# A gated recurrent layer on one core: TensorE's step loop made one loop of 128 rounds, VectorE's loop turned, weights loaded by row quarters, the opening reordered

## The reference

```
vz, vr, vh = cond @ C_z + b_z, cond @ C_r + b_r, cond @ C + b
xz, xr, xh = x @ W_z, x @ W_r, x @ W          # for every step t
h = 0
for t in range(512):
    z = sigmoid(xz[t] + h @ U_z + vz)
    r = sigmoid(xr[t] + h @ U_r + vr)
    c = tanh(xh[t] + (r * h) @ U + vh)
    h = (1 - z) * h + z * c
    out[t] = x[t] + h
```

## Time and profile before

| | |
|---|---|
| median of 3 runs | 2264.65 us (2261.95 to 2265.0) |
| the profiled execution | 2264.97 us |
| its span | 2263.1 us |
| PE busy | 2185.4 us (97%), 107502 products |
| PEld busy | 1797.5 us (79%) |
| DVE, ACT, POOL busy | 1754.5, 1326.6, 687.8 us |

### The profile page before, as it was taken

The page is one execution under the profiler, slowest core; times in us unless marked ns, Lnnn a source line. Parts: engine busy times, 40 slices in busy tenths (PEclk is TensorE's granted clock), DMA queues, the critical chain, the costliest instruction groups (busy, mean ns, idle before and its releaser), DMA issues.

```text
span 2263.1 us, 238050 instructions
## 1 busy us (share of the span) xinstructions
PE 2185.4 (97%) x107502; PEld 1797.5 (79%) x107502; DVE 1754.5 (78%) x8226; ACT 1326.6 (59%) x4623; POOL 687.8 (30%) x1546
## 2 busy tenths in 40 slices
PE   2899999999999999999999999999999999999996
PEld 1788878888888887888888888788878888888875
DVE  5687878778778777777777777777777877877874
ACT  3566556566566665666656666556656656656652
POOL 0233333333333333333333333333333333333331
PEclk9999999999999999999999999999999999999998
DMA  9110110110110110111101101101101101101101
GB/s 196 34 38 19 38 38 19 38 37 19 38 33 23 38 35 22 38 29 28 38 24 33 38 24 32 38 19 37 38 19 38 38 19 38 38 20 38 28 11 22
DMA packets 145390, 78.48 MB, mean 35 GB/s; under 512 B 9024, under 2 KB 140608, under 8 KB 145216
## 3 DMA queue, kind: packets, MB, share of 16 engines
q1 hardware_dynamic: 145216, 76.84, 14.1%
HBM read 43.25 MB, written 33.55 MB: 34 GB/s over the span
## 4 chain that ended last, share of the span: by engine, by line
PE 95%; issue 2%; SPq 1%; DMA 1%; DVE 0%; ACT 0%; DVEq 0%; POOLq 0%; POOL 0%
PE p_bank L269 44%; PE c_bank L259 20%; PE banks L297 16%; PE banks L306 15%; SPq L152 1%; DMA x_nat<-in_x_dram 1%; SPq L147 0%; SPq L163 0%; PE p_bank L278 0%; DVE taken L631 0%; DVE state L635 0%; DVE h_t L639 0%; ACT gate_c L430 0%; SPq L155 0%; DVE h_lo L597 0%
## 5 line engine op out<-in xcount | busy, mean ns | idle before, releaser
L269 PE MATMUL p_bank<-w_hi,x_t 128*32 128x384 f16 x16384 | 1183.1, 327 | 2.4 <-issue 1.6
L269 PE MATMUL p_bank<-w_lo,x_t 128*32 128x384 f16 x8192 | 701.7, 327 | 2.2 <-issue 2.2
L269 PEld LDWEIGHTS p_bank<-w_hi,x_t 128*32 128x32 f16 x16384 | 462.3, 97 | 155.2 <-issue 1.5
L259 PEld LDWEIGHTS c_bank<-u,reset_t 128*32 128x32 f32 x32704 | 488.4, 110 | 98.6 <-DVE reset_t L611 71.7
L259 PE MATMUL c_bank<-u,reset_t 128*32 128x64 f32 x32704 | 551.0, 219 | 8.4 <-issue 8.1
L230 POOL TENSOR_TENSOR result<-x_nat,state 128x128 f32<-128x128 f32 x512 | 233.9, 457 | 1010.0 <-DVE h_lo L597 1008.4
L423 ACT ACTIVATE gate_r<-banks,gates_down 128x64 f32<-128x64 f32 x1024 | 265.6, 310 | 359.1 <-PE banks L297 358.1
L430 ACT ACTIVATE gate_c<-c_bank 128x64 f32<-128x64 f32 x1024 | 228.3, 223 | 302.8 <-PE c_bank L259 302.6
L216 POOL TENSOR_TENSOR kept<-keep,state 128x128 f32<-128x128 f32 x512 | 235.7, 460 | 551.3 <-ACT keep L426 551.3
L609 DVE TENSOR_TENSOR reset<-gate_r,state 128x64 f32<-128x64 f32 x1024 | 209.0, 204 | 209.3 <-ACT gate_r L423 205.8
L419 ACT ACTIVATE h_hi<-h_t 128x64 f16<-128x64 f32 x1024 | 261.0, 255 | 148.0 <-DVE h_t L639 80.4
(11 more groups left out here) (68 smaller groups left out, 2749.6 us busy)
## 6 DMA issues: line engine op xcount, KB each, us to landing
x_nat<-in_x_dram SPq DMA_DIRECT2D x256, 128.0 KB, 3.1
out_dram<-result SPq DMA_DIRECT2D x256, 128.0 KB, 2.8
w_stage<-in_L_cond_W_r_dram SPq DMA_DIRECT2D x4, 256.0 KB, 5.4
w_stage<-in_L_cond_W_z_dram SPq DMA_DIRECT2D x4, 256.0 KB, 8.1
w_stage<-in_L_cond_W_dram SPq DMA_DIRECT2D x4, 256.0 KB, 10.8
u<-in_L_cond_U_z_dram SPq DMA_DIRECT2D x4, 256.0 KB, 13.5
u<-in_L_cond_U_r_dram SPq DMA_DIRECT2D x4, 256.0 KB, 16.0
c_w<-in_L_cond_C_r_dram SPq DMA_DIRECT2D x4, 256.0 KB, 12.7
```

Of the source, the lines that this page charges most:

```text
L259: last = nc.tensor.matmul(c_bank[part(j), a, 0:N // HALVES], reset_t[:, part(q)], u[:, C, q, half_cols(j, a)], start=False, stop=q == Q - ...
L269: last = nc.tensor.matmul(p_bank[k][part(j), 0:G * N], x_t[:, c, part(q), a], w[b][:, :, q, cols(j)], start=f == 0, stop=f == GROUPS - 1, ...
```

## The change

1. **TensorE's loop.** Steps 1 to 512 become one loop of 128 rounds of four, with a branch hint at its head. Step 512 does not exist; its waits are met by increments that VectorE and ScalarE add in their last step. The last steps run their projections too, on whatever lies in the tiles. The matrix U is waited for once ahead of the loop.
2. **70 products of zeros** of 128 columns (`WARM`) stand at the head of TensorE's code; the six clearing products of 512 columns become two of 128.
3. **VectorE's loop.** The step is cut in `begin` (low half of h, the candidate's seed) and `go_on` (the rest). A round is now `go_on` of a step and `begin` of the next, so that the loop branches back behind the seed.
4. **Loads.** A matrix is still four transfers, now one for each quarter q to all 128 partitions; cond and each bias are one transfer. The order is W_r, W_z, block 0 of x, W, cond, U_z, U_r, biases, C_r, C_z, C, U, blocks 1 to 3 of x.
5. **The opening.** VectorE takes the W scales first, x's scales behind the top of W, both U tops ahead of the first low half, and the low half of U_z behind the first `begin`. The gates' bias is scaled instead of the base. TensorE runs the products with cond ahead of the projections of steps 0 and 1. ScalarE's sum of set 2 moves into step 0.
6. **The last store.** Seven of the last eight steps are stored one step earlier, and the last step in one transfer.

```diff
+    WARM = 70
-    SPLITS = (R, Z, C, UZ, UR)
+    SPLITS = (R, Z, C, UR, UZ)
...
             def load_weights(tile, source, done):
-                rows = source.rearrange("(j q s) e -> j s q e", j=J, q=Q)
-                for p in range(J):
-                    sp.dma_start(tile[part(p)], rows[p]).then_inc(done, 16)
+                rows = source.rearrange("(j q s) e -> q j s e", j=J, q=Q)
+                for q in range(Q):
+                    sp.dma_start(tile[:, q], rows[q]).then_inc(done, 16)
...
+                if last and j == BODY - 1:
+                    sp.wait_ge(out_ready, T - 1)
+                    for p in range(J):
+                        sp.dma_start(out_rows[n, p][:, 0:BLOCK - 1], result[j % OUTS][part(p), 0:BLOCK - 1])\
+                            .then_inc(result_out[j % OUTS], 16)
+                    sp.wait_ge(out_ready, T)
+                    sp.dma_start(out_rows[n][:, :, BLOCK - 1], result[j % OUTS][:, BLOCK - 1]).then_inc(result_out[j % OUTS], 16)
+                    return
...
+            pe.wait_ge(s_zeros, 1)
+            for _ in range(WARM):
+                clear_bits(c_bank[:, 1, 0:N])
+            pe.wait_ge(s_all_sum, 1)
+            total_w(W_GATES)
+            pe.wait_ge(s_w_up, W_GATES + 1)
+            total_w(W_C)
             pe.wait_ge(s_row_sum, J + 1)
             for m in range(2):
                 total_x(1, m, 1 + m, m + 1)
...
-            step(0, 1, True, s_u_in[C])
-            with pe.Fori(0, SETS - 3) as m:
-                for tt in range(2, SET + 2):
-                    step(m, tt, False)
-            for s in range(SET * (SETS - 3) + 2, T):
-                step(s // SET, s % SET, True)
+            with nc.Fori(0, SETS, engines=[pe.engine], hint_back_edge=True) as m:
+                for tt in range(1, SET + 1):
+                    step(m, tt)
...
+            top_of_w(R)
+            top_of_w(Z)
+            scale_of_w(W_GATES)
+            top_of_w(C)
+            dve.wait_ge(s_cond_in, 16)
             V.transpose(cond_t[:], cond_nat[:]).then_inc(s_cond_t, 1)
+            scale_of_w(W_C)
             dve.wait_ge(x_totaled, 2)
...
+            top_of_w(UZ)
+            top_of_w(UR)
+            rest_of_w(0)
+            scale_of_w(U_GATES)
+            rest_of_w(1)
...
+                if last and tt == STEPS - 1:
+                    dve.sem_inc(seeded, 1)
+                    dve.sem_inc(c_seeded, 1)
+                    dve.sem_inc(h_lo_ready, HALVES)
+                    dve.sem_inc(reset_t_ready, HALVES)
...
+            begin(0, 0, True)
+            rest_of_w(4)
             with nc.Fori(0, PASSES - 1, engines=[dve.engine], hint_back_edge=True) as i:
                 for tt in range(STEPS):
-                    step(i, tt, False)
+                    go_on(i, tt, False)
+                    begin(i, tt + 1, False)
             for tt in range(STEPS):
-                step(PASSES - 1, tt, True)
+                go_on(PASSES - 1, tt, True)
+                if tt < STEPS - 1:
+                    begin(PASSES - 1, tt + 1, True)
```

More of the change, by code:

```diff
@@ L280, in total, with clear_bits @@
                 return last
[L282 to L284 removed]
+            def clear_bits(cells):
+                nc.tensor.matmul(cells, zeros[:, 0:P], zeros[:, 0:N], start=True, stop=True).then_inc(s_bits, 1)
             def total_x(k, c, of, sets):
@@ L312, in _ @@
                 total_x(1, m, 1 + m, m + 1)
[L313 to L319, removed]
+            pe.wait_ge(s_w_up, W_C + 1)
+            total_w(U_GATES)
+            pe.wait_ge(s_cond_t, 1)
+            for g in range(G):
+                pe.wait_ge(s_c_in[g], 16 * Q)
+                product(base_cell(g), cond_t, c_w[:, g], first=True).then_inc(s_base_mm, 1)
+            pe.wait_ge(s_w_up, U_GATES + 1)
+            for g in range(GATES):
+                clear_bits(cell(0, g))
             pe.wait_ge(s_w_hi, G)
@@ L324, in _, with step @@
                 project(s, s, 0, GROUPS)
[L325 to L333, removed]
             pe.wait_ge(seeded, 1)
-            pe.wait_ge(c_seeded, 1)
             pe.sem_inc(r_mm, 1)
             pe.sem_inc(z_mm, 1)
+            pe.wait_ge(c_seeded, 1)
             pe.sem_inc(c_mm, HALVES)
+            pe.wait_ge(x_t_ready, 3)
             total_x(TOTAL_STEP % 2, 0, 0, 3)
-            pe.wait_ge(x_t_ready, 3)
             project(0, 2, 0, GROUPS)
-            def step(m, tt, last, candidate_in=None):
+            pe.wait_ge(s_w_hi, len(SPLITS))
+            pe.wait_ge(s_w_lo, len(SPLITS))
+            pe.wait_ge(s_u_in[C], 16 * Q)
+            def step(m, tt):
                 s = m * SET + tt
                 c, k = tt % SET, tt % 2
[L346 to L352, removed]
+                now = pe.snap(s + 1)
+                halves = [pe.snap(HALVES * s + (a + 1)) for a in range(HALVES)]
                 pe.wait_ge(seeded, now)
@@ L439, in step @@
                 now_m = i * (STEPS // SET) + m
+                if first and tt == 0:
+                    act.wait_ge(x_in[1], 16 * J)
+                    act.wait_ge(x_summed, 2)
+                    sum_x(2, 0)
+                if t == SUM_STEP and not more(3):
+                    act.sem_inc(x_summed, 1)
                 if t == SUM_STEP and more(3):
@@ L578, in _, with begin @@
             seed_gates(0, 0)
-            dve.wait_ge(s_bits, 6)
-            def step(i, tt, last):
+            dve.wait_ge(s_bits, GATES + WARM)
+            def begin(i, tt, last):
                 s = i * STEPS + tt
@@ L604, in step, with go_on, count, more @@
                     scale_down((m + 1) % 2)
+            def go_on(i, tt, last):
+                s = i * STEPS + tt
+                m, t = divmod(tt, SET)
+                now_m = i * (STEPS // SET) + m
+                old, new = state[:, (tt - 1) % SLOTS], state[:, tt % SLOTS]
+                def count(v):
+                    return v if last else dve.snap(v)
+                now = count(s + 1)
+                def more(sets):
+                    return not (last and m + sets >= STEPS // SET)
                 for a in range(HALVES):
@@ L622, in step @@
                 dve.wait_ge(kept_ready, now)
-                if not (last and tt >= STEPS - TURN_AHEAD):
+                if last and tt >= STEPS - TURN_AHEAD:
+                    dve.sem_inc(x_t_ready, 1)
+                else:
                     ahead_m, c = divmod(tt + TURN_AHEAD, SET)
```

95 lines of the change are left out of this document (39 added, 56 removed).

## The result

The changed kernel takes 2294.79 us (median; 2294.11 to 2295.43), the kernel before 2264.31 beside it: a ratio of 1.0136, with a 95% interval of 1.0119 to 1.0154. It is slower by 1.4%, where I forecast 1.6% faster. Of the cases that I had worked out, "the loads run on four engines" is the one that came.

A forecast was written before the change was run, and what follows sets the result against it. TensorE bounds the kernel, with losses in opening, late code, VectorE's branch and last step. Opening 43.0, steps 1 to 4 24.1, steps 5 to 510 2150.4, end 9.0: 2226.5, plus 1.87 outside the span, 2228 us; range 2219 to 2306.

The forecast's parts named there:

- the loads run on four engines: Rival on weight loads: outermost count 4 deals a matrix to four engines, 12.2 to 13.8 us each; 2303 us, chance 0.22.
- The loads: Weight loads in the opening: quarters over all partitions run at 303 GB/s, 3.4 us a matrix instead of 4.64.
- The opening: Everything ahead of step 1: with faster loads step 1 starts at 43.0 us instead of 55.66, a gain of 12.7.
- the other three terms: Rest of the sum behind the opening: steps 1 to 4 24.1 us, steps 5 to 510 2150.4, the end 9.0.
- No gain from loads: Rival on weight loads: still 226 GB/s over all partitions, 12.6 us of the gain lost, 2241 us; chance 0.13.
- Steps 1 to 4: TensorE's start: 17.0 us plus six code packets at 1.19, 24.1; gain 1.2 from one packet fewer.
- Steps 5 to 510: TensorE's loop: 506 steps at 4.238 us plus six branches at 1.0, 2150.4 us.
- dearer steps: Rival in TensorE's loop: 0.02 us more in each step, for registers or the hint, 10 us, 2238; chance 0.07.
- The branch: VectorE's branch, moved behind the candidate's seed: loss about 1.0 us instead of 1.65, six times 0.65, gain 3.9.
- The end: From the start of step 511: TensorE finishes later than the output, 9.0 us instead of 11.51.
- Seven pieces of code: TensorE's loop, placed by the 70 products of zeros, fits seven pieces of 256 instructions; without them it would touch eight.
- the fear of the eighth: Rival: TensorE's loop does not stay in the engine, for instance touching eight pieces; 152 us more, 2380; chance 0.03.

The follow-up runs named there:

- The pairs: Changed kernel with weight loads of outermost count 2 (two of the four groups of 32 rows) instead of 4, eight transfers a matrix: 2386.03 us.
- loads by 32 rows: Changed kernel with the nine matrices loaded as before, one transfer for each j to 32 partitions: 2241.70 us, ratio 0.9904.
- two queues: Changed kernel, weights, cond and biases by 32 rows, SyncE loading partitions 0 to 63, ScalarE 64 to 127: 2235.76 us; with both queues in the same order 2227.58.
- all partitions: Changed kernel with each quarter 128 evenly spaced rows, outermost count 128 on both sides, output not the reference's: 2228.91 us, ratio 0.9849.
- the kernel without the turn: Changed kernel with loads by 32 rows and VectorE's branch back at the end of a whole step, as before: 2253.43 us, ratio 0.9952.

## Why the prediction was wrong

**The loads, the step that failed.** I took 303 GB/s, 3.4 us a matrix, "because what the change alters is where neighbours write". The change alters a second thing, how many engines write, and this one I made a rival at 0.22 although it had a written rule and a count of packets on its side, and I had myself noted that nothing in the trace spoke against it. The pairs show it: with the count halved, so is the rate. A matrix took 10.7 us. The opening is 114.42 instead of the 43.0 of my sum, so 71.4 us more; the other three terms are 4.3 better together. My range, 2219 to 2306, holds the result only because I had stretched it to this rival's price; that is no merit of the forecast.

**The rival's own price** was 2303 to 2315, and the result is 2294.8. Its mechanism was right and its size was not: I gave four engines a quarter of 303 to 345 GB/s, 76 to 86. They moved 98 to 100, since each of them was faster than I had taken it. By rate and share, with 16 engines: 226 / (1.08 x 16) = 13.1 GB/s for an engine before, 13.3 with loads by 32 rows, 18 to 21 with two queues, 14 to 22.7 with all partitions, 98 / (0.26 x 16) = 23.6 for one of four, and 49 / (0.13 x 16) = 23.6 for one of two. Whether it is the few engines or the other partitions that they write, these kernels do not separate. Nine matrices at 10.7 are 96 us instead of 110 to 124. The point from which it decides, 7.3 us a matrix, was passed.

**The rate with all engines.** "No gain from loads" (226 GB/s, 2241) is what the changed kernel gives with loads by 32 rows: 2241.7, at 188 to 228 GB/s. That the times agree is luck, for its step 1 starts 6 us later than in my sum for that case (61.6 against 55.6) and its steps are 6 us better. With 16 engines over all partitions the windows up to 38 us give 239 to 385, in the mean 285. My 303 was somewhat above that, and the span of that kernel is 2226.6 where my sum was 2226.5. This is luck too, for the terms cancel: its step 1 starts at 49.1 instead of 43.0, since W_r is there at 7.8 and not at 5.4 and VectorE waits another 3.28 us for W_z, and its steps are some 6 us better.

**Steps 1 to 4:** 24.1 forecast, 22.9 measured. TensorE's code comes in eight packets, none behind step 4, where I had written about nine. Five of the first round's six come in these steps and one ahead of them, and 1.2 us is the price that I had put on one packet.

**Steps 5 to 510:** 2150.4 forecast, 2147.3 measured, with TensorE busy for 2145.28 of it. No rival of dearer steps: the steps without a branch are 4.22 and 4.27 us, as before.

**The branch.** The term was mis-sized: a loss of 1.0 a time was forecast, some 0.5 came. Timeline around it in the changed kernel:

```profile
387.78 0.35 DVE L514 SCALAR_TENSOR_TENSOR c_bank<-p_bank,x_down,base 128x128 f32<-128x128 f32 x1
...
389.01 0.23 DVE L628 TENSOR_TENSOR reset<-gate_r,state 128x64 f32<-128x64 f32 x1 [0.88 <-ACT gate_r L423]
...
389.57 0.65 PE L265 MATMUL c_bank<-u,reset_t 128*32 128x64 f32 x32
```

From the seed's start to `reset` it is 1.23 us, where I had put 1.87; in a step without the branch it is 0.84. The wait is named after `gate_r`, but ScalarE began that at 388.26, so `reset` starts 0.75 us behind it. In the step of the earlier trace rows it is 0.35 (327.58 to 327.93). The 0.4 us more are what the branch adds. Why it takes less here than behind `h_t` no run shows. The six steps are 4.58 to 4.87 us, and the kernel without the turn puts the worth of the turn in these steps at 6.9 us, where I had 3.9.

**The end:** 9.0 forecast, 8.96 measured, TensorE last as I had it. The last issue of the store is 3.5 us ahead of TensorE's last products:

```profile
2289.42 0.64 SPq L178 DMA_DIRECT2D out_dram<-result  x1
...
2292.96 0.35 PE L275 MATMUL p_bank<-w_hi,x_t 128*32 128x384 f16 x4
```

**Seven pieces of code.** The count was right, the fear of the eighth was not: with 10 zeros nothing changes.

## What to carry to other kernels

Before a transfer is cut anew, write down its outermost count on both sides: in this kernel a count of 4 moved 98 to 100 GB/s, where a count of 32 onto a quarter of the partitions moved 188 to 228, and it holds up whatever the queue has behind it, small transfers too. When a rule for a shape is at hand and the trace has no such shape, the rule is the forecast and not a rival. To write more partitions at a time, keep 32 rows to a transfer and give the halves of the partitions to two queues, in the order in which they are needed: here that gave 306 to 356 GB/s up to 28 us.

## What the runs showed of the hardware that I had not expected

By rate and share, a single DMA engine moves 23.6 GB/s as one of two or four and up to 22.7 as one of sixteen over all partitions, against 13.1 as one of sixteen onto 32 partitions. Four engines therefore give 43% of what sixteen give onto 32 partitions at a time (98 against 226 GB/s), not a quarter. A single transfer of biases with four rows as its outermost count holds SyncE for 1.5 to 4.6 us, and four transfers of the same bytes, in the same place of the queue, for 1.8. And VectorE is idle for 0.88 us around the branch behind the candidate's seed, against 1.59 to 1.63 behind the last transpose of h.
